# Cross-attention and FFN on one core: the front half in another order, context keys and values first, queries last

## What is computed

```
x: (8, 112, 1024)   ctx: (8, 375, 1024)      32 query heads, 4 key/value heads, head size 128
h = layernorm(x)
q = h @ Wq ; k, v = concat(ctx, h) @ Wk, @ Wv     # keys and values: 375 of the context, 112 of the latents
x = x + softmax(q k^T / sqrt(128)) v @ Wo
x = x + layernorm_affine(shared_ffn(n) + routed_ffn(n)),   n = layernorm(x)
```

## Time and profile before

| what | value |
|---|---|
| median of 3 runs | 1890.15 us (1890.11 to 1891.3) |
| profiled execution | 1891.63 us |
| its span, first to last instruction | 1889.8 us |
| PE busy | 1833.2 us (97%), 9246 matmuls |
| DVE, ACT, POOL busy | 633.9, 606.3, 608.5 us |
| mean granted PE clock | 0.987 |
| DMA | 245.67 MB, mean 130 GB/s |

### The profile page before, as it was taken

How to read it: one execution, slowest core, us unless ns; L and a number is a source line. 1 busy time by engine, 2 the same in 40 slices (tenths; PEclk the granted TensorE clock), 3 DMA queues, 4 the chain that set the end, 5 groups by cost and what they waited for, 6 DMA issues and landing times.

```text
span 1889.8 us, 26387 instructions
## 1 busy us (share of the span) xinstructions
PE 1833.2 (97%) x9246; PEld 1616.5 (86%) x9246; DVE 633.9 (34%) x1096; ACT 606.3 (32%) x1149; POOL 608.5 (32%) x392
## 2 busy tenths in 40 slices
PE   6999999999999997999999999999999999999996
PEld 5999998888888876888888888988888988888886
DVE  6112111111111125731772277147534432211216
ACT  3222222211111125731772277137523213212321
POOL 2322223311111105542453255225456322222242
PEclk8999999999999998999999999999999999999998
DMA  4665644643433443422342144124335231111134
GB/s 172 203 231 205 212 155 156 207 157 139 139 139 139 171 169 125 164 97 74 123 151 80 63 155 143 67 94 144 100 123 178 90 101 56 56 55 46 55 100 167
DMA packets 107880, 245.67 MB, mean 130 GB/s; under 512 B 22464, under 2 KB 67520, under 8 KB 106816
## 3 DMA queue, kind: packets, MB, share of 16 engines
q1 hardware_dynamic: 102624, 234.64, 36.2%
q10 hardware_dynamic: 5216, 10.49, 1.6%
HBM read 168.30 MB, written 76.81 MB: 130 GB/s over the span
## 4 chain that ended last, share of the span: by engine, by line
PE 47%; issue 38%; POOL 13%; DVE 1%; ACT 1%; POOLq 1%; ACTq 0%; DVEq 0%
PE bank L1163 15%; PE bank L1164 15%; PE bank L1165 15%; POOL tile_region L639 8%; POOL slab_split L602 4%; PE bank L1197 1%; ACT slab_split L674 0%; POOL y_region L647 0%; DVE small L898 0%; DVE mid_region L891 0%; POOLq L638 0%; POOLq L606 0%; ACT mid_region L684 0%; POOLq L649 0%; DVE tile_region L1135 0%
## 5 line engine op out<-in xcount | busy, mean ns | idle before, releaser
L602 POOL TENSOR_TENSOR slab_split<-slab_raw,slab_split 128x1024 fp32r<-128x1024 f32 x134 | 324.2, 2420 | 711.1 <-ACT slab_split L674 711.1
L1163 PE MATMUL bank<-act_region,slab_split 128*128 128x448 f32 (+2 forms) x1376 | 504.1, 366 | 10.7 <-POOL slab_split L602 6.6
L1165 PE MATMUL bank<-act_region,slab_split 128*128 128x448 f32 (+2 forms) x1376 | 503.1, 366 | 0.0
L1164 PE MATMUL bank<-act_region,slab_split 128*128 128x448 f32 (+2 forms) x1376 | 502.7, 365 | 0.0
L639 POOL TENSOR_TENSOR tile_region<-tile_region,small 128x488 f32<-128x488 f32 x224 | 216.3, 1002 | 284.9 <-DVE small L975 284.9
L1163 PEld LDWEIGHTS bank<-act_region,slab_split 128*128 128x128 f32 x1376 | 260.0, 189 | 39.3 <-POOL slab_split L602 7.9
L1164 PEld LDWEIGHTS bank<-act_region,slab_split 128*128 128x128 f32 x1376 | 260.0, 189 | 25.5
L1165 PEld LDWEIGHTS bank<-act_region,slab_split 128*128 128x128 f32 x1376 | 259.7, 189 | 25.0
L674 ACT ACTIVATE slab_split<-slab_raw 128x1024 fp32r<-128x1024 f32 x134 | 141.7, 1058 | 415.7 <-PE bank L1165 382.5
L1163 PE MATMUL bank<-mid_region 122*128 122x448 f32 (+1 forms) x480 | 199.0, 415 | 1.6 <-ACT tile_region L797 1.1
L1012 DVE TENSOR_TENSOR y_region<-y_region,bank 128x512 f32 (+2 forms) x96 | 59.6, 621 | 365.5 <-PE bank L1165 365.5
(11 more groups left out here) (98 smaller groups left out, 2277.7 us busy)
## 6 DMA issues: line engine op xcount, KB each, us to landing
slab_raw<-in_slabs SPq DMA_DIRECT2D x134, 512.0 KB, 3.5
q_scratch<-y_region SPq DMA_DIRECT2D x16, 1792.0 KB, 8.5
mid_region<-q_scratch SPq DMA_DIRECT2D x32, 896.0 KB, 5.6
v_scratch<-y_region SPq DMA_DIRECT2D x8, 2048.0 KB, 7.4
mid_region<-v_scratch SPq DMA_DIRECT2D x32, 512.0 KB, 3.6
k_scratch<-small_region SPq DMA_DIRECT2D x32, 488.0 KB, 3.1
mid_region<-k_scratch SPq DMA_DIRECT2D x32, 488.0 KB, 6.4
tile_region<-in_ctxT SPq DMA_DIRECT2D x8, 1500.0 KB, 10.7
```

The costliest lines, as they stand in the source:

```text
L602: pool.tensor_tensor(WS[s][1], RAWS[s], f32(WS[s][0]), ALU.subtract).then_inc(s_wlo, 1)
L1163: pe.matmul(out_ap, w[0], a[0], start=first, stop=False)
L1164: pe.matmul(out_ap, w[0], a[1], start=False, stop=False)
L1165: return pe.matmul(out_ap, w[1], a[0], start=False, stop=last)
```

## The change

The front half is written anew; the attention and the FFN keep their work.

- PE's order becomes: context keys and values of all 8 batches; among the products of the last batch and of the first latent keys, the transposes of the latents; the latent keys (4 heads, two halves of 448 rows); the latent values (8 batches); all 32 query heads in one loop.
- The first batch is done piece by piece: 4 phases of key products and 4 of value products, each for one piece of Wk or Wv as it comes. ACT and DVE split pieces and quarters of the first context.
- Context units now have N = 376 (keys, 375 and one pad) and 3 tiles of 125 rows (values) instead of 488 and 4 tiles of 122. The latents are transposed in 16 groups of 4 with 112 rows. Seven PSUM banks are used for units, the eighth for the transposes.
- XT isn't stored and loaded back. Keys of context and latents have scratch arrays of their own, so that an attention step loads q, two parts of k and two parts of v: 5 DMAs instead of 3, with the latent keys in rows of 448 bytes.
- The half-slab positions (`EDGE`) are gone: 32 slabs are loaded and split for the queries, not 40.
- After head 11 SP loads q, k and v of the first two attention steps (10 DMAs) between the store of heads 10 and 11 and the load of slab 14.
- PE's transposes of the probabilities have 125 stationary columns, not 122; the normalise of POOL has 487 columns, not 488.

```
-SLAB_AT = (2 * list(range(EDGE)) + list(range(EDGE, NH - EDGE)) + 2 * list(range(NH - EDGE, NH)) ...
+SLAB_AT = (list(range(T_FC1)) + list(range(T_FC1 - NK, T_FC1)) ...
+SEG1 = [g for u in range(N_CTX - 1) for g in (("ln", u), ("ctx", u))] + [("ln", 6), ("ln", 7), ("ctx", N_CTX - 1)] + [
+    g for m in range(NKV) for g in (("ln", 8 + 2 * m), ("ln", 9 + 2 * m), ("kl", m, 0))] + [
+    ("kl", m, 1) for m in range(NKV)] + [("vl", b) for b in range(B)]
...
 SP
+            for k in range(4):
+                if k == 3:
+                    sp.dma_start(CRAW[:, 2 * k:2 * k + 2, :], ctxT[0, :, 2 * k:2 * k + 2, :]).then_inc(s_first[k], 16)
+                    sp.wait_ge(s_plo, 1)
+                sp.dma_start(PRAW[k % 3], wkv[k]).then_inc(s_piece[k % 3], 16)
+                if k < 3:
+                    sp.dma_start(CRAW[:, 2 * k:2 * k + 2, :], ctxT[0, :, 2 * k:2 * k + 2, :]).then_inc(s_first[k], 16)
+            for k in range(4, NK):
+                sp.wait_ge(s_plo, k - 2)
+                sp.dma_start(PRAW[k % 3], wkv[k]).then_inc(s_piece[k % 3], 16)
+            sp.wait_ge(s_flo, 4)
+            sp.dma_start(CRAW, ctxT[1]).then_inc(s_ctx, 16)
+            for b in range(B):
+                sp.dma_start(X8[0:SQ, b, :], x[b * SQ:(b + 1) * SQ, :]).then_inc(s_x, 16)
...
+            def next_ctx(b):
+                sp.wait_ge(s_clo, b)
+                sp.dma_start(CRAW, ctxT[b + 1]).then_inc(s_ctx, 16)
+            store_ctx(0)
+            with sp.Fori(1, B - 1) as b:
+                next_ctx(b)
+                store_ctx(b)
...
+            def q_pair(kv, g, m):
+                for s in range(2):
+                    load_slab(m + s + 2, s, m + s + 2)
+                store_pair(kv, g, C_Q + 2 * m + 3, g // 2 % 2)
...
+            q_heads(0)
+            for g in range(0, 4, 2):
+                q_pair(1, g, G + g)
+            sp.wait_ge(s_vst, FREE + 16 * B)
...
+            for n in range(2):
+                load_qk(0, n, n, n)
+                load_v(0, n, n, n)
+            for g in range(4, G, 2):
+                q_pair(1, g, G + g)
 ACT
+            for k in range(4):
+                piece_hi(k)
+                act.wait_ge(s_first[k], 16)
+                act.activation(HT[0][:, 0, 2 * k:2 * k + 2, 0:SC], CRAW[:, 2 * k:2 * k + 2, :], ACT.Copy).then_inc(s_fhi, 1)
...
+            for s in range(2):
+                act.wait_ge(s_vlst[s], 16 * B // 2)
+            with act.Fori(0, NH // 4) as i:
+                for r in range(4):
+                    slab_hi(4 * i + r + 1, (r + 1) % 2, C_Q + 8 * i + 2 * r)
 DVE
+            for k in range(NK):
+                dve.wait_ge(s_phi, k + 1)
+                dve.tensor_tensor(piece(k, 1), PRAW[k % 3], f32(piece(k, 0)), ALU.subtract).then_inc(s_plo, 1)
+                if k < 4:
+                    ks = slice(2 * k, 2 * k + 2)
+                    dve.wait_ge(s_fhi, k + 1)
+                    dve.tensor_tensor(HT[0][:, 1, ks, 0:SC], CRAW[:, ks, :], f32(HT[0][:, 0, ks, 0:SC]),
+                                      ALU.subtract).then_inc(s_flo, 1)
...
 PE
+            for j in range(4):
+                pe.wait_ge(s_plo, j + 1)
+                pe.wait_ge(s_flo, j + 1)
+                for u in range(NKV):
+                    ctx_step(u, 0, 2 * j)
+                    last = ctx_step(u, 0, 2 * j + 1)
...
+            def ctx_product(b, u, j, between=None):
+                pe.wait_ge(s_ev, N_CTX * b + u - N_CTX + 1)
+                for k in range(NK):
+                    if k == 4 and between is not None:
+                        ln_group(between)
+                    last = ctx_step(u, j, k)
+                last.then_inc(s_mm, 1)
```

More of the change, by code:

```diff
@@ L278, in xattn_ffn @@
         SB, AV = bank[0:3], bank[5:7]
-        order = [GB[(C_WO + j) % 4] for j in range(4)]
+        order = [GB[(C_WO - C_Q + j) % 4] for j in range(4)]
         LAST_USE = [j for j in range(4) if order[j] is not bank[5]]
@@ new lines, in _ @@
+            ctx_hi(1, 1, None)
+            act.wait_ge(s_pad, 3)
+            for u in range(N_CTX):
+                ctx_unit_hi(0, u)
+            ctx_hi(2, 0, N_CTX)
+            for u in range(N_CTX):
+                ctx_unit_hi(1, u)
+                sqrt_var(u, u, SQ)
+            sqrt_var(B - 1, B - 1, SQ)
+            with act.Fori(1, B // 2 - 1) as i:
+                for j in range(2):
+                    ctx_batch(2 * i + j, j)
+            ctx_batch(B - 2, 0)
+            n = C_LAT - N_CTX
@@ L973, in reciprocal_sums @@
+            with dve.Fori(0, NH // 4) as i:
+                for r in range(4):
+                    for h in range(2):
+                        q_lo(C_Q + 8 * i + 2 * r + h, C_Q + 2 * r + h, h, r % 2, r // 2)
             def reciprocal_sums(n, first, end):
@@ L1218, in _ @@
-            with pe.Fori(0, (NH - 2 * EDGE) // 2) as i:
+                    if SEG1[j - 1][0] != "ln":
+                        ln_group(g[1])
+                    continue
+                if g[0] == "ctx":
+                    ctx_product(B - 1, g[1], 1, second)
+                elif g[0] == "kl":
+                    _, m, h = g
+                    pe.wait_ge(s_ev, n - N_CTX + 1)
+                    pe.wait_ge(s_lnlo, 8 * h + 8)
+                    for k in range(NK):
+                        if k == 4 and second is not None:
+                            ln_group(second)
+                        last = k_step(unit_bank(n)[:, 0:HALF], lambda l, k: XT[h][:, l, k, :], m, k)
+                    last.then_inc(s_mm, 1)
+                else:
+                    b = g[1]
+                    pe.wait_ge(s_ev, n - N_CTX + 1)
+                    cols = slice(b % 4 * SQ, (b % 4 + 1) * SQ)
+                    for k in range(NK):
+                        last = v_step(unit_bank(n)[0:SQ, :], lambda l, k: XT[b // 4][:, l, k, cols], k)
+                    last.then_inc(s_mm, 1)
@@ L1252, in av @@
+            pe.wait_ge(s_pad, 6)
             def av(s, a, ts):
```

624 lines of the change are left out of this document (271 added, 353 removed).

## The result

The changed kernel takes 1878.96 us (median of 4 runs, 1875.88 to 1879.83), the kernel before in the same session 1890.13 (1889.34 to 1891.3): a ratio of 0.9937, with a 95% interval from 0.9920 to 0.9955. The forecast was 1877.6. The profiled execution of the changed kernel took 1878.53 with a span of 1876.7 (forecast: 1879.1 and 1877.3); the two profiled spans, 1889.8 and 1876.7, are 13.1 us apart, more than the medians' 11.2, because the profiled execution before was 1.5 us above its median.

A forecast was written before the change was run, and what follows sets the result against it. PE, busy 97%, bounds the kernel, so only its idle time, slow clock or matmuls can yield time. 32.5 us goes and 20.0 comes, 12.5 less: 1877.6 us for the median, range 1868 to 1887.

The forecast's parts named there:

- the stall at slab 14: After head 11, ten loads ahead of the slab make PE 5.0 us late, plus 2.2 of slow clock; chance 0.50.
- no stall: Rival: the ten loads don't delay slab 14 enough to stall PE; 1870.4 us, chance 0.22.
- (a): Goes: 19.2 us lost before PE's first product. Comes: 10.7 for a start at 8.8 plus slow clock.
- (b): Goes: 1.9 us of slow clock behind the start. Comes: latent transposes take 7.2 against 5.6 before, +1.6.
- (c): Goes: 1.35 us idle in 40 to 80. Comes: context loop, 33.1 us a batch, loads covered, cost 0.
- (d): Goes: 6.5 us at Q2's end, slab load behind a store. Comes: 0.5 from latent values to queries.
- (e): Goes: 3.5 us of idle and slow clock in 320 to 360. Comes: 7.2 from ten loads before slab 14.
- (f): Comes: two more load issues in attention leave 3.8 us of cover for key loads; cost 0.
- Everything dear: Rival: slow burst +4.8, fixed matmul cost +2.7, waiting start phases up to +4; 1880.3 to 1889 us, chance 0.14.
- The context loop: Rival: the store, load, ACT and POOL chain outgrows a 33 us batch; 1889.6 us, chance 0.05.
- Weight loads set the pace: Rival: 376-column matmuls keep the 202.5 ns of the 448s, costing 24.6 us; 1902.2 us, chance 0.04.
- Keys late: Rival: small latent-key rows delay landings in attention beyond 3.8 us of cover; 1907.6 us at one microsecond over, chance 0.05.

The follow-up runs named there:

- the kernels in which the stall was taken away: Changed kernel with slabs 14 and 15 issued ahead of all ten loads, 1869.75 us, or with five of the loads moved behind the slabs, 1868.96 us.
- the late start: Changed kernel with TensorE waiting at the start for all four first pieces of weights and context; 1885.6 us against 1878.6.
- the swapped load: Kernel before, with the third query group's slab issued ahead of the second group's last store; 1883.29 us, 6.9 less.
- the cut-up operation: Kernel before with the third group's slab issued early, and VectorE's low part of the first context batch cut in three; 1881.07 us, 2.2 less than without the cut.
- the kernel with the slabs ahead: Changed kernel with slabs 14 and 15 issued ahead of the ten loads; 1869.75 us, 8.85 less than the changed kernel.
- the wider keys: Changed kernel with the context keys' moving side 440 columns wide instead of 376, the added ones zeros; 1901.36 us, 22.8 more.
- the zeroing in pieces: Changed kernel with GpSimd zeroing the y region in eight pieces between batches and the gate's region behind the first key head; 1862.07 us, 16.5 less.
- the repeat of the changed kernel: The changed kernel unaltered, timed again in the first experiment session; 1878.6 us, its profiled execution 1875.21.
- the four variants of the changed kernel without the stall: All ten loads behind the slabs (1869.75 us), five behind (1868.96), all ten behind plus zeroing in pieces (1855.43), all ten behind plus doubled latent transposes (1876.31).

## Why the prediction was right

**Its sum.** 12.5 us off was forecast, 11.2 measured between the medians, and the range held it. The first score was forecast at 686 and came at 687.28 and at 684.08, for the two paces. The likeliest case, the stall at slab 14, is the one that happened; the price of *no stall* (1870.4) was met by the kernels in which the stall was taken away, at 1869.75 and 1868.96.

**What goes.** (a), (b): that the start counts one for one was assumed, and the late start shows it within about a microsecond. (c): 1.35 idle is gone, not tried by itself. (d): 6.5 against 6.7 in the profiles of the swapped load. (e): the size read from the trace was right (1.9 idle, 1.6 of slow clock) and its reason, "the same", wrong: GpSimd was slowed by VectorE, as the cut-up operation shows, and its slow clock hung on the first stall. The change took it away all the same. Why is argued from its order and tried by no run: it has no half-slab positions, and its long passes of the context don't lie beside a slab that is wanted 4.86 us later.

**What comes.** (a) 10.0 against 10.7: start at 7.63, not 8.8 (and before the 8.5 to 10 that was given as a sign of being right), since the table load lay before the data; the slow clock until 12.78 held 16 matmuls at 313 instead of 172 ns, 2.3 us where 1.9 stood. (b) By the trace 16 x 0.40 = 6.4 against 7.2 for all the transposes, a price by the piece as taken. (c) Zero: the trace has no idle of PE in the context loop, a batch takes 33.35 us (forecast 33.1), and 376 columns take 172.2 ns instead of 170.5, 768 x 1.7 = 1.3 us more than was summed. (d) ACT takes slab 1 after waiting 4.78 us for the last value store, and PE doesn't wait; 0.5 was put down. (e) 4.63 idle and 9 matmuls at 373 ns instead of 206, 1.5 us: 6.1 against 7.2. The rate of 0.445 MB/us with a margin gave ACT's take of the slab to 0.4 us. The Trainium skill (DMA: Bandwidth & Descriptors, Queues, rings and completion order) has a DMA engine take one ring's descriptors in ring order; the trace agrees: behind ten loads the slab was taken at S + 19.2, behind five at S + 14.3. (f) No wait on a load in the attention.

**What it missed.** Behind the stall the query products kept the pace of 206.7 ns in the profiled execution and, by their times, in six of the nine of the changed kernel: 36 x 0.1 = 3.5 us. It lies in no term, and it is why taking the stall away gave 8.85 us, more than the 6.1 that the hole and the slow clock hold. It was hidden by the small errors of the other terms: start -0.7, transposes -0.8, columns +1.3, latent values -0.5, burst -1.1, which with +3.5 make +1.7, against the +1.0 by which the first score came late (687.28 against 698.74 - 12.5). That the forecast came so near is to that extent luck. The attention's own first wait, 11.2 us, stood in both traces and was rightly taken as unchanged; the 1.7 us less behind the first score were not forecast. Most of them are the clock: the windows of the 10 us behind the end of that wait, of the changed kernel and of the kernel before, have a mean clock of 0.85 and of 0.75,

```profile
709.50:719.50 10.00, 9.99 (x48) 9.16 (x49) 7.46 (x15) 7.29 (x19) 1.80 (x2) 0.85 0.01 2
721.08:731.08 10.00, 10.00 (x44) 8.82 (x45) 7.30 (x13) 6.54 (x17) 0.92 (x1) 0.75 0.00 0
```

so 1.5 and 2.5 us are lost there, 1.0 of the 1.7. In the kernel with the slabs ahead, whose way from the first score to the end takes 1.5 us longer than the changed kernel's (1190.9), the same window has 0.72. The other 0.7 is open.

**The rivals.** *Everything dear*: its slow burst and its waiting phases did not come; of its fixed cost per matmul about half did (7.7 ns; the 1.3 us of (c) above). *The context loop*: it stayed covered, but less safely than the prediction had it. GpSimd ended a batch's low part some 12 us before PE wanted it in the later batches, 8 in the first two, and in the third only 2.7, here at 107.36, with PE's batch beginning at 110.09:

```profile
101.27 6.09 POOL L591 TENSOR_TENSOR act_region<-tile_region,act_region 128x3000 fp32r<-128x3000 f32 x1 [32.33 <-ACT act_region L687]
110.09 0.33 PE L1114 MATMUL bank<-act_region,mid_region 128*128 128x376 f32 x1
```

That context was issued 11.1 us after its batch began (87.80 against 76.74), where a later one goes after 2.7 (112.74 against 110.09); the statistics of the latents, between which ACT waited on DVE until 89.04, stand in that stretch. *Weight loads set the pace*: refuted, 172.2 ns at 376 columns. *Keys late*: the landings took 5.5 (context) and 5.9 us (latents) at the median against 6.4 before, and PE waited for none.

## What to carry to other kernels

A queue's order is part of a schedule: before a burst of loads is put into a queue, ask which small load behind it is wanted next, and when. Here ten loads cost 9 us ahead of two slabs and nothing behind them. Where TensorE is full on both sides of a hole, every microsecond at its start and in its holes counts, and a hole can cost more than its length: add the slow clock (it came behind the holes of 4.3 to 4.7 us here, but not behind the one of 1.90 by itself), and look whether the pace behind it is the old one. An engine's wait for a whole region's memset is worth a look in every kernel; this one, untouched by the change, held 14.3 us, more than the 11.2 that the change brought.

## What the runs showed of the hardware that was not expected

- **Two paces at full clock.** The same matmuls of 448 columns stand 202.7 or 206.7 ns apart, for 170 us on end, at a granted clock of 1.00. The slower one was seen only behind a stall, in four of the five profiles that have the stall at slab 14 (the changed kernel, the late start, the wider keys, the zeroing in pieces); the fifth, the repeat of the changed kernel, has the faster pace. None of the four variants of the changed kernel without the stall showed it, and their runs spread by at most 1.1 us, those with it by 3.3 to 5.2. The kernel before has holes of 4.32 and 1.90 us and no slower pace behind them, and its runs spread too (by 3.9 us in fourteen), so a spread alone doesn't tell of the pace. What picks the pace isn't settled: the slow clock behind the stall held 9, 9, 16 and at least 15 matmuls in the four and 11 in the fifth, which tells nothing.
- **Weight loads.** The records give a load of 128 or 125 columns 188 ns and yet a distance of 172 ns between matmuls of 376 columns, each with its own load. Here a load's recorded time was no bound on the pace.
- **The slow clock behind equal waits differs.** Behind some 4.6 us of idle it held 9 matmuls in one execution of the changed kernel and 11 in the other; behind 1.90 us it came in the kernel before, with another stall 24 us ahead of it, and not when that stall was gone.
